# Five blocks of attention and feed-forward on one core: the two P·V steps of a group are set apart, and V's products move between them

## The chip, the cores and the metric

The kernel runs on one core of a Trainium2 chip. The metric is the device time of one execution in microseconds (us), the median of several runs. A profiled execution has a span (first to last instruction) and a time of its own beside it.

## What is computed

Input x has 32 sequences of 64 rows with 128 columns, the context 32 x 64 rows with 96 columns. Five stages follow one another, all in float32:

```python
x = attn(ln(x, g1, b1), ln(x, g1, b1), Wq1, Wk1, Wv1, Wo1, bo1) + x   # SELF: 16 heads of 64
x = attn(ln(x, g2, b2), context, Wq2, Wk2, Wv2, Wo2, bo2) + x         # CROSS: keys and values of the context
x = geglu_ff(ln(x, g3, b3)) + x                                       # GEGLU
# block 2: attention over the context with 16 heads of 8 (CROSS2), then a feed-forward part (FFN)
...
def attn(xq, xc, ...):
    q, k, v = xq @ Wq, xc @ Wk, xc @ Wv       # 16 heads of 64
    P = softmax(q @ k.T * 64 ** -0.5)         # per sequence and head, 64 x 64
    return (P @ v) @ Wo + bo
```

## The kernel before

The 2048 rows are cut into 8 groups of 256 rows, each of T = 2 tiles of 128 rows (two sequences a tile). The stages SELF and CROSS go over the groups one after another. Every engine has its own program, written out in order, and they meet at semaphores alone: an engine does its rows in the order of the code, and a wait at one row holds up everything behind it on that engine. No planner sets the order.

In group s, `one` is the next group and `two` the one after it (a CROSS group follows the last SELF group). TensorE's program of a SELF or CROSS group is: turn P of tile 0 (`turn_step(s, 0)`, 8 transpositions of 128x128), turn the finished output of the group before, turn x (and the context) of `two` (`x_step`), turn P of tile 1, P times V of both tiles (`av_step`, 64 x 64 matmuls, 64 for each tile), three of the four V products of `one` (`val_step`, three float32r matmuls of 512 columns each), the scores of `one` (`scores_step`, 64x64 matmuls), the output projection (`out_step`), the q and k projections of `two` (`proj_step`, 48 matmuls of 256 columns), and the fourth V product of `one`. The high and the low part of float32r operands are multiplied apart, hence the threes.

What comes out of TensorE lies in PSUM. The scores, the turned P and P·V of tile t all use the banks 2t and 2t+1 of `scp`; everything else that is staged (x, projections, V) goes round three banks `stage0` to `stage2`, each of which is free again when the copies of the product three places earlier are done (`stage_for`). ScalarE (ACT) and VectorE (DVE) copy these results to SBUF: of the turned P one bank each (`pt_step`, into `pt`), of V's products 0, 1 and 3 one half each, of V's product 2 both halves by ACT (`copiers`). The softmax of tile t is a chain: DVE takes the maximum (L1298) and subtracts it (L1303), ACT exponentiates (L1071), DVE sums (L1331) and inverts (L1333), GpSimd (POOL) multiplies by the inverse (L1582) and signals `probs`; only then may `turn_step(s, t)` begin. `av_step(s, t)` waits for the V copies of that tile and for both copies into `pt` of that tile.

`Counts` counts the semaphore values in the order of the program, so that it has to be changed along with the engines.

Of the kernel before, what the change touches and what calls it, by code (L numbers as in the profile page):

```python
# [38 lines left out]
SELF, CROSS, GEGLU, CROSS2, FFN = range(5)  # L39
# [54 lines left out]
class Counts:  # L94


    def __init__(self):
        self.total, self.value, self.uses, self.start = {}, {}, [], {}
        self.x(SELF, 0)
        self.p(SELF, 0)  # L100
        self.x(SELF, 1)
        for t in range(T):
            self.softmax(SELF, 0, t)
        self.p(SELF, 1)
        self.vals(SELF, 0, range(4))
        for p in range(PHASES):
            for g in range(GROUPS):
                self.group(p, g)
# [49 lines left out]
    def group(self, p, g):  # L158
        self.start[("act", p, g)] = self.total["act"]
        self.start[("dve", p, g)] = self.total["dve"]  # L160
        self.start[("uses", p, g)] = len(self.uses)
        one, two = Step(p, g).ahead(1), Step(p, g).ahead(2)
        if p in (SELF, CROSS):
            for t in range(T):
                self.turned(p, g, t)
            if one.phase == GEGLU:
                for t in range(T):
                    self.p(GEGLU, 0, (2 + t,))
                    for i in range(2):
                        self.use("av", p, g, 2 * t + i)  # L170
                self.p(GEGLU, 1, (0, 1))
                self.x(GEGLU, 2)
                self.use("down", GEGLU, 0)
                self.p(GEGLU, 1, (2, 3))
            else:
                self.x(two.phase, two.first)
                for i in range(4):
                    self.use("av", p, g, i)
                self.vals(one.phase, one.first, range(3))
                for t in range(T):  # L180
                    self.softmax(one.phase, one.first, t)
                if two.phase == GEGLU:
                    self.vals(one.phase, one.first, (3,))
                    self.x(GEGLU, 1)
                    self.p(GEGLU, 0, (0, 1))
                else:
                    self.p(two.phase, two.first)
                    self.vals(one.phase, one.first, (3,))
            for name in ("out_turned", "out_copied", "out0", "added"):
                self.tick(name, (p, g))  # L190
        elif p == CROSS2:
            last = one.phase != CROSS2
            if g > 0:
                for i in (2, 3):
                    self.use("pt", p, g - 1, i)
            if not last:
                self.qk(p, g + 1)
                self.use("v", p, g + 1)
                if two.phase == CROSS2:
                    self.x(two.phase, two.first)  # L200
            self.tick("scores", (p, g))
            for t in range(T):
                self.softmax(p, g, t)
            for i in (0, 1):
                self.use("pt", p, g, i)
            if g > 0:
                self.use("at", p, g - 1)
                self.use("wo", p, g - 1)
            if not last and two.phase == FFN:
                self.x(two.phase, two.first)  # L210
            for name in ("out0", "norm", "atted"):
                self.tick(name, (p, g))
            if last:
                for i in (2, 3):
                    self.use("pt", p, g, i)
                self.p(one.phase, one.first, (0, 1))
                self.x(two.phase, two.first)
                self.use("at", p, g)
                self.p(one.phase, one.first, (2, 3))
                self.use("wo", p, g)  # L220
        elif (p, g) != (GEGLU, 0):
            if one:
                self.p(one.phase, one.first, (0, 1))
            if two:
                self.x(two.phase, two.first)
            if one and one.phase == p:
                self.p(one.phase, one.first, (2, 3))
            self.use("down", p, g)
# [37 lines left out]
def attention_blocks(nc, w, out):  # L266
# [3 lines left out]
    with ctx:  # L270
# [323 lines left out]
        def _(pe):  # L594
# [315 lines left out]
            def group(s):  # L910
                one, two = s.ahead(1), s.ahead(2)
# [9 lines left out]
                if s.phase in (SELF, CROSS):  # L921
# [4 lines left out]
                    if before:  # L926
                        out_turn_step(before)
                    x_step(two, s)
                    turn_step(s, 1)
                    av_step(s, 0)  # L930
                    av_step(s, 1)
                    val_step(one, range(3), s)
                    scores_step(one, 0)
                    scores_step(one, 1)
                    out_step(s, 0)
# [1 line left out]
                    if two.phase == GEGLU:  # L937
                        val_step(one, (3,), s)
                        x_step(s.ahead(3), s)
                        p_step(two, s, (0, 1))  # L940
                    else:
                        proj_step(two, s)
                        val_step(one, (3,), s)
                elif s.phase == CROSS2:


# [48 lines left out]
            scores_step(Step(SELF, 0), 0, range(6, PAIRS))  # L995
            scores_step(Step(SELF, 0), 1)
            proj_step(Step(SELF, 1), None)
            val_step(Step(SELF, 0), range(4))
            each_group(pe, group)


# [1 line left out]
        def _(sc):  # L1003
# [137 lines left out]
            def group(s):  # L1141
                one, two = s.ahead(1), s.ahead(2)
# [5 lines left out]
                if s.phase in (SELF, CROSS):  # L1148
                    pt_step(s, 0)
                    x_turned_step(two)  # L1150
                    pt_step(s, 1)
                    av_step(s, 0)
                    av_step(s, 1)
                    val_step(one, range(3))
                    x_high_step(two)
                    for key, first in (("q", 3), ("k", 4), ("v", 5)):
                        if s.is_group(SELF, first):
# [10 lines left out]
                    if two.phase == GEGLU:  # L1168
                        val_step(one, (3,))
                        exp_step(one, 1)  # L1170
                    else:
                        p_step(two, range(2))
                        exp_step(one, 1)
                        p_step(two, range(2, 8))
                        val_step(one, (3,))
                elif s.phase == CROSS2:
                    before, last = s.before(), one.phase != CROSS2
                    if before:
# [43 lines left out]
            p_step(Step(SELF, 1), range(1, 5))  # L1222
            exp_step(Step(SELF, 0), 1)
            p_step(Step(SELF, 1), range(5, 8))
            val_step(Step(SELF, 0), range(4))
            each_group(sc, group)


        @block.vector
        def _(ve):  # L1230
# [174 lines left out]
            def group(s):  # L1405
# [7 lines left out]
                if s.phase in (SELF, CROSS):  # L1413
# [5 lines left out]
                    pt_step(s, 0)  # L1419
                    if before:  # L1420
                        out_step(before)
                    pt_step(s, 1)
                    stats_step(three)
                    av_step(s, 0)
                    av_step(s, 1)
                    val_step(one, (0,))
                    max_step(one, 0)
                    shift_step(one, 0)
                    if two.phase != GEGLU:
# [6 lines left out]
                    if two.phase == GEGLU:  # L1436
                        probs_step(one, 0)
                    sum_step(one, 1)
                    if two.phase != GEGLU:
                        val_step(one, (3,))  # L1440
                    if three.is_group(GEGLU, 0):
                        stats_step(s.ahead(4))
                elif s.phase == CROSS2:
# [60 lines left out]
            sum_step(Step(SELF, 0), 0)  # L1504
            p_step(Step(SELF, 1), range(4, 8))
            sum_step(Step(SELF, 0), 1)
            val_step(Step(SELF, 0), range(4))
            each_group(ve, group, looks_far=True)


# [199 lines left out]
```

## Time and profile before

| | |
|---|---|
| median of 3 runs | 456.05 us (454.42 to 456.29) |
| profiled execution: time / span | 456.08 us / 454.4 us |
| TensorE busy | 438.6 us, 97% of the span |
| VectorE, ScalarE, GpSimd busy | 355.0 us (78%), 320.0 us (70%), 198.1 us (44%) |
| granted TensorE clock | 1.00 |

The share of busy time is an average over the whole span. SELF and CROSS together take the part from about 26 to 302 us.

### The profile page before, as it was taken

How to read it: one execution, taken by the hardware profiler on the slowest of the kernel's cores; microseconds unless marked ns; L12 is line 12 of the kernel's file. 1: busy time of each engine (PE TensorE's matmuls, PEld its weight loads, DVE VectorE, ACT ScalarE, POOL GpSimd, SP SyncE). 2: the span in 40 equal slices, each digit the busy share in tenths (PEclk: the TensorE clock that was granted, in tenths of full speed). 3: DMA queues.
4: the chain of work that ended last, by engine and by line, in shares of the span. 5: the costliest groups of instructions: out<-in, count | busy, mean ns of one | idle time of the engine just before them, and what ended most of it. 6: DMA issues, size and time to landing. Idle time of an engine off the chain costs nothing.

```text
span 454.4 us, 17380 instructions
## 1 busy us (share of the span) xinstructions
PE 438.6 (97%) x7545; PEld 403.5 (89%) x7545; DVE 355.0 (78%) x653; ACT 320.0 (70%) x589; POOL 198.1 (44%) x220
## 2 busy tenths in 40 slices
PE   7999999999999999999999999999999999999897
PEld 7979999898998999999989899888999777877797
DVE  4888889688797897887968879896774787898571
ACT  5686676776878768777776777875565576766763
POOL 2793332565455535553354433533332231232583
PEclk9999999999999999999999999999999999999999
DMA  7102021110200000000000000000000000000011
GB/s 227 47 15 84 3 84 30 50 48 7 60 3 4 10 12 2 12 3 10 12 4 10 3 12 12 4 1 1 3 0 19 10 20 11 0 1 3 13 36 46
DMA packets 14621, 10.57 MB, mean 23 GB/s; under 512 B 5188, under 2 KB 13592, under 8 KB 14552
## 3 DMA queue, kind: packets, MB, share of 16 engines
q1 hardware_dynamic: 14120, 9.48, 7.3%
q8 instruction: 56, 0.92, 0.8%
q10 hardware_dynamic: 432, 0.07, 0.1%
q14 instruction: 13, 0.11, 0.1%
HBM read 8.50 MB, written 1.05 MB: 21 GB/s over the span
## 4 chain that ended last, share of the span: by engine, by line
PE 85%; DVE 7%; ACT 4%; issue 2%; DMA 1%; POOL 0%; DVEq 0%; ACTq 0%; POOLq 0%
PE stage L637 12%; PE stage L638 11%; PE stage L639 11%; PE scp L812 7%; PE scp L733 7%; PE scp L886 6%; PE scp L782 6%; PE out0p L832 4%; PE out0p L834 3%; PE out0p L833 3%; PE out0p L858 3%; PE stage L796 2%; PE scp L750 2%; DVE pr L1303 1%; DVE mx L1298 1%
## 5 line engine op out<-in xcount | busy, mean ns | idle before, releaser
L1582 POOL TENSOR_TENSOR pr<-pr,rc 128x1024 f32<-128x1024 f32 (+1 forms) x32 | 59.1, 1866 | 76.9 <-DVE rc L1333 76.8
L1071 ACT ACTIVATE pr<-pr 128x1024 f32<-128x1024 f32 x48 | 50.8, 1059 | 37.7 <-DVE pr L1303 29.9
L1521 POOL TENSOR_TENSOR rstd<-veps,neghalf 128x2 f32<-128x2 f32 x32 | 22.7, 710 | 78.0 <-DVE veps L1251 77.9
L1005 ACT ACTIVATE vt<-stage 64x512 f32<-64x512 f32 x83 | 49.2, 592 | 4.7 <-PE stage L639 1.2
L1347 DVE COPY vt<-stage 64x512 f32<-64x512 f32 x45 | 31.2, 694 | 21.8 <-PE stage L639 20.9
L1298 DVE TENSOR_REDUCE mx<-scp 128x16 f32<-128x1024 f32 x32 | 39.2, 1224 | 9.0 <-PE scp L733 8.5
L1005 ACT ACTIVATE ot_h<-scp 128x512 fp32r<-128x512 f32 x64 | 33.5, 601 | 13.4 <-PE scp L812 13.4
L1353 DVE TENSOR_TENSOR ot_r<-scp,ot_h 128x512 fp32r<-128x512 f32 x64 | 40.0, 684 | 2.4 <-ACT ot_h L1005 1.0
L1005 ACT ACTIVATE k_of_heads<-stage 128x512 f32<-128x512 f32 x62 | 36.9, 597 | 5.6
L1303 DVE TENSOR_TENSOR pr<-scp,mx 128x1024 f32<-128x1024 f32 x32 | 39.2, 1225 | 1.1
L1331 DVE TENSOR_REDUCE sm<-pr 128x16 f32<-128x1024 f32 x32 | 38.0, 1188 | 0.0
L812 PEld LDWEIGHTS scp<-pt,vt 64*64 64x64 f32 x2048 | 32.4, 135 | 5.9 <-issue 5.6
L812 PE MATMUL scp<-pt,vt 64*64 64x64 f32 x2048 | 34.9, 221 | 2.7 <-issue 1.6
L733 PEld LDWEIGHTS scp<-k_of_heads,q_of_heads 64*64 64x64 f32 x2048 | 31.5, 135 | 6.2 <-issue 5.7
L733 PE MATMUL scp<-k_of_heads,q_of_heads 64*64 64x64 f32 x2048 | 33.9, 220 | 0.6 <-issue 0.6
L782 PE MATMUL scp<-ident,pr 128*128 128x128 f32 x256 | 33.7, 274 | 0.2 <-POOL pr L1582 0.2
L1595 POOL TENSOR_TENSOR masked_k<-kT,fourmask 128x1024 f32<-128x1024 f32 x8 | 15.1, 1893 | 42.9 <-ACT kT L1050 42.9
L1005 ACT ACTIVATE q_of_heads<-stage 128x512 f32<-128x512 f32 x49 | 27.5, 589 | 7.5 <-PE stage L639 7.0
L782 PEld LDWEIGHTS scp<-ident,pr 128*128 128x128 f32 x256 | 29.0, 140 | 3.2 <-POOL pr L1582 0.5
L1358 DVE COPY pt<-scp 128x512 f32<-128x512 f32 x32 | 22.1, 692 | 9.6 <-PE scp L782 9.6
L1005 ACT ACTIVATE pt<-stage 128x512 f32<-128x512 f32 x32 | 17.9, 595 | 9.3 <-PE stage L796 8.7
L1537 POOL TENSOR_TENSOR rows<-rows,bias 128x256 f32<-128x256 f32 (+1 forms) x32 | 23.3, 731 | 1.2
(257 smaller groups left out, 1408.9 us busy)
## 6 DMA issues: line engine op xcount, KB each, us to landing
ctx_in<-in_ctx_dram SPq DMA_DIRECT2D x16, 96.0 KB, 2.0
masked_k<-in_L_xattn_Wo_dram SPq DMA_DIRECT2D x2, 512.0 KB, 3.8
out_dram<-rows SPq DMA_DIRECT2D x8, 128.0 KB, 1.8
rows<-in_x_dram SPq DMA_DIRECT2D x1, 768.0 KB, 9.5
pr<-in_L_xattn_Wq_dram SPq DMA_DIRECT2D x1, 512.0 KB, 4.6
pr<-in_L_xattn_Wk_dram SPq DMA_DIRECT2D x1, 512.0 KB, 6.2
pt<-in_L_xattn_Wv_dram SPq DMA_DIRECT2D x1, 512.0 KB, 7.6
rows<-in_L_xattn_Wq_dram SPq DMA_DIRECT2D x1, 512.0 KB, 3.7
```

Source lines behind the costliest of these rows:

```text
L637: nc.tensor.matmul(dst, wh, mh, start=start, stop=False)
L638: nc.tensor.matmul(dst, wh, mr, start=False, stop=False)
L639: return nc.tensor.matmul(dst, wr, mh, start=False, stop=True)
L733: last = nc.tensor.matmul(scp[64 * b:64 * b + 64, 2 * t + e, a * N:(a + 1) * N], heads_of[0][h, a, n], heads_of[1][h, a, n], start=True, s ...
L782: last = nc.tensor.transpose(scp[:, 2 * t + c, q * 128:(q + 1) * 128], pr[t][:, a * 128:(a + 1) * 128], ident[:, :])
L812: last = nc.tensor.matmul(banks[i][64 * e:64 * e + 64, m * ROWS + b * N:m * ROWS + (b + 1) * N], vt[h, 2 * t + b, (2 * m + e) * DH:(2 * m ...
L1005: return nc.scalar.activation(dst, s, ACT.Copy)
L1071: nc.scalar.activation(pr[t][:, :], pr[t][:, :], ACT.Exp, scale=scale[s.phase]).then_inc(exped, 1)
L1298: nc.vector.tensor_reduce(mx[:, t, :], sc3, AX.X, ALU.max).then_inc(maxed, 1)
L1303: nc.vector.tensor_tensor(halves(pr[t][:, :]), sc3, mx[:, t, :, None].to_broadcast([ROWS, H, N]), ALU.subtract).then_inc(shifted, 1)
L1353: nc.vector.tensor_tensor(ot_r[:, :, i, t, :], bank, of.bitcast(F32), ALU.subtract).then_inc(dve, 1)
L1582: nc.gpsimd.tensor_tensor(p, p, rc[:, t, h:, None].to_broadcast([ROWS, H - h, N]), ALU.mult)\
```

## The change

The fourth V product of a group, which stood at the end of the group before, now stands inside its own group, behind the turn of `two`'s x. P·V of tile 0 follows it; only then comes the turn of P of tile 1, then the first V product of the next group, P·V of tile 1, and the V products 1 and 2. The last SELF/CROSS group that uses this code (CROSS, 6) keeps its successor's fourth product where it was. ACT and DVE copy in the new order; on DVE the statistics of group `three` move ahead of the second copy of the turned P. No instruction is added to any engine and none is removed.

```diff
--- before.py
+++ after.py
@@ -102,7 +102,7 @@
         for t in range(T):
             self.softmax(SELF, 0, t)
         self.p(SELF, 1)
-        self.vals(SELF, 0, range(4))
+        self.vals(SELF, 0, range(3))
         for p in range(PHASES):
             for g in range(GROUPS):
                 self.group(p, g)
@@ -174,9 +174,12 @@
                 self.p(GEGLU, 1, (2, 3))
             else:
                 self.x(two.phase, two.first)
+                self.vals(p, g, (3,))
                 for i in range(4):
+                    if i == 2:
+                        self.vals(one.phase, one.first, (0,))
                     self.use("av", p, g, i)
-                self.vals(one.phase, one.first, range(3))
+                self.vals(one.phase, one.first, (1, 2))
                 for t in range(T):
                     self.softmax(one.phase, one.first, t)
                 if two.phase == GEGLU:
@@ -185,7 +188,6 @@
                     self.p(GEGLU, 0, (0, 1))
                 else:
                     self.p(two.phase, two.first)
-                    self.vals(one.phase, one.first, (3,))
             for name in ("out_turned", "out_copied", "out0", "added"):
                 self.tick(name, (p, g))
         elif p == CROSS2:
@@ -926,10 +928,12 @@
                     if before:
                         out_turn_step(before)
                     x_step(two, s)
+                    val_step(s, (3,), s)
+                    av_step(s, 0)
                     turn_step(s, 1)
-                    av_step(s, 0)
+                    val_step(one, (0,), s)
                     av_step(s, 1)
-                    val_step(one, range(3), s)
+                    val_step(one, (1, 2), s)
                     scores_step(one, 0)
                     scores_step(one, 1)
                     out_step(s, 0)
@@ -940,7 +944,6 @@
                         p_step(two, s, (0, 1))
                     else:
                         proj_step(two, s)
-                        val_step(one, (3,), s)
                 elif s.phase == CROSS2:
 
 
@@ -995,7 +998,7 @@
             scores_step(Step(SELF, 0), 0, range(6, PAIRS))
             scores_step(Step(SELF, 0), 1)
             proj_step(Step(SELF, 1), None)
-            val_step(Step(SELF, 0), range(4))
+            val_step(Step(SELF, 0), range(3))
             each_group(pe, group)
 
 
@@ -1148,10 +1151,12 @@
                 if s.phase in (SELF, CROSS):
                     pt_step(s, 0)
                     x_turned_step(two)
+                    val_step(s, (3,))
                     pt_step(s, 1)
                     av_step(s, 0)
+                    val_step(one, (0,))
                     av_step(s, 1)
-                    val_step(one, range(3))
+                    val_step(one, (1, 2))
                     x_high_step(two)
                     for key, first in (("q", 3), ("k", 4), ("v", 5)):
                         if s.is_group(SELF, first):
@@ -1172,7 +1177,6 @@
                         p_step(two, range(2))
                         exp_step(one, 1)
                         p_step(two, range(2, 8))
-                        val_step(one, (3,))
                 elif s.phase == CROSS2:
                     before, last = s.before(), one.phase != CROSS2
                     if before:
@@ -1222,7 +1226,7 @@
             p_step(Step(SELF, 1), range(1, 5))
             exp_step(Step(SELF, 0), 1)
             p_step(Step(SELF, 1), range(5, 8))
-            val_step(Step(SELF, 0), range(4))
+            val_step(Step(SELF, 0), range(3))
             each_group(sc, group)
 
 
@@ -1419,11 +1423,12 @@
                     pt_step(s, 0)
                     if before:
                         out_step(before)
+                    val_step(s, (3,))
+                    stats_step(three)
                     pt_step(s, 1)
-                    stats_step(three)
                     av_step(s, 0)
+                    val_step(one, (0,))
                     av_step(s, 1)
-                    val_step(one, (0,))
                     max_step(one, 0)
                     shift_step(one, 0)
                     if two.phase != GEGLU:
@@ -1436,8 +1441,6 @@
                     if two.phase == GEGLU:
                         probs_step(one, 0)
                     sum_step(one, 1)
-                    if two.phase != GEGLU:
-                        val_step(one, (3,))
                     if three.is_group(GEGLU, 0):
                         stats_step(s.ahead(4))
                 elif s.phase == CROSS2:
@@ -1504,7 +1507,7 @@
             sum_step(Step(SELF, 0), 0)
             p_step(Step(SELF, 1), range(4, 8))
             sum_step(Step(SELF, 0), 1)
-            val_step(Step(SELF, 0), range(4))
+            val_step(Step(SELF, 0), range(3))
             each_group(ve, group, looks_far=True)
```

On TensorE, group SELF 6 (V's products read `wv_of0`, here `src0` for the group's own product 3 and `src1` for those of SELF 7), from the last V product ahead of the turns to the scores. Before:

```order
L637 MATMUL stage<-wv_of0h,src0h 128x512
L638 MATMUL stage<-wv_of0r,src0h 128x512
L639 MATMUL stage<-wv_of0h,src0r 128x512
L782 MATMUL scp<-ident,pr 128x128 x8
L843 MATMUL out0p<-ident,attT 128x128 x2
L648 MATMUL stage<-ident,ctx_in 96x128 x2
L655 MATMUL stage<-ident,xn 128x128 x2
L782 MATMUL scp<-ident,pr 128x128 x8
L812 MATMUL scp<-pt,vt 64x64 x64
L637 MATMUL stage<-wv_of0h,src1h 128x512
```

The same place in the changed kernel (its lines are numbered two higher):

```order
L784 MATMUL scp<-ident,pr 128x128 x8
L845 MATMUL out0p<-ident,attT 128x128 x2
L650 MATMUL stage<-ident,ctx_in 96x128 x2
L657 MATMUL stage<-ident,xn 128x128 x2
L639 MATMUL stage<-wv_of0h,src0h 128x512
L640 MATMUL stage<-wv_of0r,src0h 128x512
L641 MATMUL stage<-wv_of0h,src0r 128x512
L814 MATMUL scp<-pt,vt 64x64 x32
L784 MATMUL scp<-ident,pr 128x128 x8
L639 MATMUL stage<-wv_of0h,src1h 128x512
L640 MATMUL stage<-wv_of0r,src1h 128x512
L814 MATMUL scp<-pt,vt 64x64 x32
```

The first turn now follows the projections at once, and the one run of 64x64 matmuls (a row of this view counts them by twos: x64 stands for 128) is now two runs, with 128x128 matmuls between them.

On VectorE, the same group, from the last reciprocal of SELF 6's softmax to the first maximum of SELF 7's. Before:

```order
L1333 RECIPROCAL rc<-sm 128x16
L1347 COPY vt<-stage 64x512
L1358 COPY pt<-scp 128x512
L1365 TENSOR_TENSOR rows<-out0p,rows 128x256
L1358 COPY pt<-scp 128x512
L1242 BN_STATS stats<-rows 128x6 x2
L1246 COPY seen<-stats 128x1
L1248 BN_AGGR mv<-stats 128x2 x2
L1251 TENSOR_SCALAR veps<-mv 128x2
L1353 TENSOR_TENSOR ot_r<-scp,ot_h 128x4x128 x4
L1347 COPY vt<-stage 64x512
L1298 TENSOR_REDUCE mx<-scp 128x16
```

In the changed kernel, from behind the reciprocal (its lines are numbered four higher):

```order
L1362 COPY pt<-scp 128x512
L1369 TENSOR_TENSOR rows<-out0p,rows 128x256
L1351 COPY vt<-stage 64x512
L1246 BN_STATS stats<-rows 128x6 x2
L1250 COPY seen<-stats 128x1
L1252 BN_AGGR mv<-stats 128x2 x2
L1255 TENSOR_SCALAR veps<-mv 128x2
L1362 COPY pt<-scp 128x512
L1357 TENSOR_TENSOR ot_r<-scp,ot_h 128x4x128 x2
L1351 COPY vt<-stage 64x512
L1357 TENSOR_TENSOR ot_r<-scp,ot_h 128x4x128 x2
L1302 TENSOR_REDUCE mx<-scp 128x16
```

The copy of the V product and the statistics now stand ahead of the second copy into `pt`, and another V copy stands between the two pairs of P·V's remainders.

## Rows read from the trace of the kernel before

**Rows 1.** The page: the chain that ended last, share of the span by engine

```profile
PE 85%; DVE 7%; ACT 4%; issue 2%; DMA 1%; POOL 0%; DVEq 0%; ACTq 0%; POOLq 0%
```

**Rows 2.** Busy time by group: window, length, each engine's us (instructions), clock, DMA

```profile
81.35:100.82 19.47, 18.80 (x363) 17.29 (x361) 15.45 (x25) 14.34 (x26) 9.57 (x9) 1.00 0.11 33
100.82:119.84 19.02, 18.43 (x362) 17.06 (x360) 15.45 (x25) 14.33 (x25) 9.69 (x9) 1.00 0.14 39
119.84:137.97 18.13, 18.13 (x362) 16.95 (x361) 15.36 (x25) 14.15 (x25) 9.41 (x9) 1.00 0.01 3
137.97:156.32 18.35, 18.35 (x364) 17.17 (x362) 15.35 (x25) 14.71 (x27) 10.21 (x10) 1.00 0.04 8
...
229.76:249.27 19.51, 18.62 (x364) 17.30 (x363) 15.46 (x25) 14.01 (x26) 7.86 (x9) 1.00 0.03 8
249.27:268.07 18.80, 18.52 (x364) 17.18 (x363) 15.45 (x25) 13.91 (x26) 7.97 (x9) 1.00 0.03 8
```

**Rows 3.** Timeline of TensorE, group SELF 6: start, length, line, operation

```profile
137.27 0.40 PE L637 MATMUL stage<-wv_of0h,src0h 128*128 128x512 f32 x1
...
137.97 1.03 PE L782 MATMUL scp<-ident,pr 128*128 128x128 f32 x8
138.84 0.38 PE L843 MATMUL out0p<-ident,attT 128*128 128x128 f32 x2
...
139.49 1.04 PE L782 MATMUL scp<-ident,pr 128*128 128x128 f32 x8
140.46 2.12 PE L812 MATMUL scp<-pt,vt 64*64 64x64 f32 x128
142.51 0.50 PE L637 MATMUL stage<-wv_of0h,src1h 128*128 128x512 f32 x1
142.85 0.39 PE L638 MATMUL stage<-wv_of0r,src1h 128*128 128x512 f32 x1
143.08 0.40 PE L639 MATMUL stage<-wv_of0h,src1r 128*128 128x512 f32 x1
...
144.46 0.39 PE L639 MATMUL stage<-wv_of0h,src1r 128*128 128x512 f32 x1
144.78 2.10 PE L733 MATMUL scp<-k_of_heads,q_of_heads 64*64 64x64 f32 x128
...
156.32 1.03 PE L782 MATMUL scp<-ident,pr 128*128 128x128 f32 x8
```

**Rows 4.** Timeline of VectorE, group SELF 6

```profile
140.57 0.69 DVE L1358 COPY pt<-scp 128x512 f32<-128x512 f32 x1 [0.51 <-PE scp L782]
141.17 0.48 DVE L1242 BATCH_NORM_STATS2 stats<-rows 128x6 f32<-128x128 f32 x2
...
142.03 0.17 DVE L1251 TENSOR_SCALAR veps<-mv 128x2 f32<-128x2 f32 x1
...
146.01 1.23 DVE L1298 TENSOR_REDUCE mx<-scp 128x16 f32<-128x1024 f32 x1 [0.50 <-PE scp L733]
...
153.49 0.25 DVE L1333 RECIPROCAL rc<-sm 128x16 f32<-128x16 f32 x1
...
156.52 0.69 DVE L1347 COPY vt<-stage 64x512 f32<-64x512 f32 x1 [1.41 <-PE stage L639]
```

**Rows 5.** Timeline of GpSimd: one product by the inverse, and a pair of them

```profile
135.47 1.90 POOL L1582 TENSOR_TENSOR pr<-pr,rc 128x1024 f32<-128x1024 f32 x1 [4.00 <-DVE rc L1333]
...
153.82 3.77 POOL L1582 TENSOR_TENSOR pr<-pr,rc 128x1024 f32<-128x1024 f32 x2 [3.25 <-DVE rc L1333]
```

**Rows 6.** Timeline of two places where TensorE waited: CROSS 6 and CROSS 7

```profile
288.39 0.69 DVE L1358 COPY pt<-scp 128x512 f32<-128x512 f32 x1
...
289.23 0.47 PE L812 MATMUL scp<-pt,vt 64*64 64x64 f32 x17 [0.41 <-DVE pt L1358]
...
301.28 1.55 POOL L1582 TENSOR_TENSOR pr<-pr,rc 128x512 f32<-128x512 f32 x1 [4.60 <-DVE rc L1333]
...
302.89 0.33 PE L782 MATMUL scp<-ident,pr 128*128 128x128 f32 x1 [0.24 <-POOL pr L1582]
```

## The prediction, made before the changed kernel ran

> **What bounds the kernel now.** I read the chain that ended last first: 85% of it is TensorE [rows 1]. An average can hide stages, so the busy time by group comes next: in the groups of SELF and CROSS from 119.84 and from 137.97, TensorE's busy time is the whole window (18.13 of 18.13 us, 18.35 of 18.35), while VectorE has 15.36 and 15.35 and the others less [rows 2]. At full clock throughout, every us added to TensorE's stream there is a us of the kernel, and there are next to no waits left to take away. The exceptions are four groups with pauses, which the profile puts down to issue and not to another engine: 19.47 and 19.02 against 18.13, 19.51 and 18.80 against 18.35, together 3.8 us [rows 2].
>
> A second loop runs close behind it. From the start of the scores (144.78) TensorE comes to the next turn at 156.32, 11.54 us later [rows 3]. The softmax of tile 0 goes the same way round: the maximum starts at 146.01, the reciprocal at 153.49 [rows 4], GpSimd at 153.82, and one product by the inverse takes 1.90 [rows 5]; so P of tile 0 is ready at 155.72, and TensorE takes up such a result 0.06 us after it (301.28 + 1.55 = 302.83, and the turn starts at 302.89) [rows 6]. That makes 155.78, or 11.00 us after the start of the scores: 0.54 us of cover. VectorE's share of this can't shrink, since it works through from the maximum to the sums, and the change leaves its rows there in their order.
>
> **The change, term by term, in one group.** The instructions are the same 364, so only their neighbours and the waits change.
>
> 1. The switch between 128x128 and 64x64 matmuls. The eight turns of tile 0 take 0.87 us to the next row (137.97 to 138.84), the eight of tile 1, with P·V behind them, 0.97 (139.49 to 140.46): 0.10 for going into 64x64. Behind P·V the first V matmul takes 0.34 to the next (142.51 to 142.85) where the second takes 0.23: 0.11 for coming out. V to scores is the same again, 0.32 against 0.23 [rows 3]. Before there are two runs of 64x64 matmuls in a group, P·V and scores; after there are three, as P·V is cut in two. One way in and one way out more: 0.21 us. The program has no semaphore ahead of that first V matmul that was late, so a wait doesn't explain the 0.11.
>
> The Trainium skill (TensorEngine Tiling (Array Packing), Key Properties) says that changing the tiling mode, not just the tile, drains TensorE. By that rule the switch costs in both directions, as these rows show; taken as a whole turn in flight on the way in, it would be 0.16 (a turn is 0.27 us long and follows the last in 0.11) in place of my 0.10, and the 15 groups would cost 0.9 us more. The rows measure the switch itself, so the sum goes by them.
>
> 2. P·V of tile 1 waits for the copy of its turned P. The copy by VectorE starts 1.08 us after the start of turn 1 (139.49 to 140.57) and takes 0.69 [rows 4]; a P·V that was held up by such a copy starts 0.15 behind its end (288.39 + 0.69 = 289.08, and 289.23) [rows 6]. So P·V of tile 1 can't start before 1.92 us after turn 1, besides the 0.11 of the switch ahead of that turn, which is counted in term 1. TensorE has 0.87 of turns and one V product between, 0.70 (137.27 to 137.97), and 0.10 for the switch: 1.67 [rows 3]. The wait is 0.25 us. Before, 64 matmuls of P·V of tile 0, 1.0 us, were the cover, plus the switch; the V product alone is 0.3 shorter. The copy must also find VectorE free. Ahead of it stand now the V copy and the statistics. By the rows, the V product ends 2.22 us after turn 0 (1.52 + 0.70), its copy at about 3.1, the statistics take 1.03 (141.17 to 142.20) and end at 4.1, and the copy is due at 4.5. That fits by 0.4. The P·V copies of tile 1 end at about 8.4 after turn 0, the second scores need them at 9.0, and the maximum starts at 9.2: no new wait there.
>
> 3. The first turn waits for `probs`. With the fourth V product gone from its front, TensorE reaches it 11.54 - 0.70 = 10.84 us after the scores, and P is ready after 11.00: 0.16 us of wait. The wait stands first in the group, so all of TensorE's work of the group is behind it. Turn 1, on the other hand, comes 1.8 us later than before while its P is ready 1.87 after tile 0's: no wait.
>
> 4. The V product itself moves by 0.70 us inside the loop and costs the same. Its bank needs the copies of the projection three places earlier, and VectorE had idled 1.41 us ahead of its copy [rows 4]: nothing is late.
>
> A second way to the same sum is the loop: turn 0 to scores was 6.81 (137.97 to 144.78) and becomes 6.81 + 0.70 + 0.21 + 0.25 = 7.97; scores to turn 0 becomes 11.00. The group is 18.97 us where it was 18.35: +0.62. The new waits add up and don't cover one another, since each is met at another place of one loop.
>
> **The sum.** Terms 1 and 2 fall in 15 groups (SELF 0 to 7, CROSS 0 to 6): 15 x 0.46 = 6.9. Term 3 falls in the 14 of them that follow another: 14 x 0.16 = 2.2. Back come the 0.41 us that TensorE waited in CROSS 6 [rows 6], where the copy of turned P stood behind the statistics and a V copy that is gone now. In SELF 0 two small waits may change places; I count nothing. Together +8.7. The profiled execution has 456.08 us (span 454.4), which is the median of the runs (456.05), so the forecast is 465.
>
> **Bounds.** Term 1 is measured four times and lies between 0.18 and 0.24: 2.7 to 3.6. Term 2 is nothing if VectorE's copy starts earlier than before relative to its turn (0), and 0.4 if VectorE is late by as much again; I take 0.25 because start and length of the copy are the same operation on the same tile. Term 3 is nothing if anything speeds up the chain by 0.16, and 0.3 if GpSimd's signal takes as long to act as VectorE's 0.15. All at the low end: +2.3 to +2.7; all at the high end: about +13.
>
> **The rivals.**
> (a) Only the switches count: a moment's slack in the two waits that I work out to tenths. For it: 0.25 and 0.16 are differences of large numbers. Against it: they come from the same steady loop, repeated 14 times. 15 x 0.21 gives 3.2, less 0.4: 459. Chance 0.17.
> (b) The pauses go. They fall into or right after the dense runs of 64x64 matmuls, and these are now shorter. With my terms: 465 - 3.8 = 461. For it: 128 matmuls in a run are 64 now. Against it: the scores keep their run, and two of the four pauses (100.82, 249.27) are not in P·V's share of their group as far as I can tell from windows. Chance 0.12.
> (c) The other side, faster: the same pauses go and the switch and both waits are hidden, 456.1 - 3.8 - 0.4 = 452. It decides only from the point at which the added cost of a group is below 0.13 us (15 x 0.13 = 2, and 0.5% is 2.3 us); one switch each way is more than that already. Chance 0.04.
> (d) No difference: P·V behind a semaphore that is met late hides its own switch, and somewhere 0.4 us of a group is given back that I don't see: 456. Chance 0.07.
> (e) More: VectorE, moved closer to its limit, delays the second copy or the scores by another 0.3 us in each group, 15 x 0.3 = 4.5: 469. It decides if the statistics end later than 4.5 us after turn 0, 0.4 more than worked out. Chance 0.08.
> The forecast itself has 0.52, with a range of 462 to 467.5.
>
> **How the numbers follow.** The range 459 to 468 holds the forecast, (b) and most of (a), and leaves out (c), (d) and most of (e). A measurement of this kernel tells about 0.5%, 2.3 us, from no change. Faster by more: (c), 0.04. Within: (d) and the low part of (a), 0.10. Slower: the rest, 0.86.
>
> **What would show it.** Right: groups of about 18.9 to 19.0 us from turn 0 to turn 0; three places in a group where TensorE's pitch has the extra 0.1; P·V of tile 1 with a wait on VectorE's copy into `pt`; the first turn of a group with a short wait on GpSimd; TensorE's busy share below that of before. Wrong: first turns that follow the projections without a gap (term 3), P·V of tile 1 that starts 1.7 us after turn 1 (term 2), no extra pitch at the second run of 64x64 (term 1), or groups without pauses at all (b).

## The result, and the profile after

The changed kernel takes 464.11 us (463.72 to 464.22, 4 runs) against 455.64 (454.42 to 456.29, 4 runs) on the same chip: 1.0187 of the time before, 95% interval 1.0163 to 1.0211. That is 8.5 us slower; 465 was forecast, in a range of 459 to 468.

The page of the changed kernel, its chain that ended last, answers to [rows 1]:

```profile
span 462.4 us, 17382 instructions
...
PE 445.4 (96%) x7545; PEld 401.9 (87%) x7545; DVE 359.6 (78%) x653; ACT 320.7 (69%) x589; POOL 198.2 (43%) x220
...
PE 80%; DVE 13%; ACT 3%; issue 2%; DMA 1%; POOL 0%; DVEq 0%; ACTq 0%; POOLq 0%
```

TensorE is still the bound, but VectorE's share of the chain is 13% where it was 7%: TensorE now waits for it in every group. The span is 8.0 us longer.

Busy time by group in the changed kernel, from turn 0 to turn 0, answers to [rows 2]:

```profile
82.84:102.04 19.20, 19.03 (x362) 17.00 (x362) 15.53 (x25) 14.34 (x25) 9.56 (x9) 1.00 0.12 40
102.04:121.43 19.39, 18.82 (x360) 17.02 (x360) 15.63 (x25) 14.32 (x24) 9.55 (x9) 1.00 0.14 38
121.43:140.34 18.91, 18.74 (x363) 16.90 (x361) 15.53 (x25) 14.24 (x25) 9.56 (x9) 1.00 0.01 3
140.34:159.44 19.10, 18.93 (x363) 17.11 (x363) 15.53 (x25) 14.83 (x26) 10.23 (x10) 1.00 0.03 8
255.07:274.17 19.10, 18.91 (x362) 17.10 (x363) 15.53 (x25) 13.87 (x25) 7.87 (x9) 1.00 0.03 8
```

A regular group that turns a context (SELF 6 to CROSS 5) takes 19.10 us instead of 18.35, one without takes 18.90 instead of 18.20. The long groups with pauses, up to 19.5 us before, are nearly gone: the longest is the one of 19.39 us.

The timeline of TensorE in SELF 6 of the changed kernel answers to [rows 3]:

```profile
140.34 1.09 PE L784 MATMUL scp<-ident,pr 128*128 128x128 f32 x8
141.27 0.38 PE L845 MATMUL out0p<-ident,attT 128*128 128x128 f32 x2
...
142.38 0.40 PE L641 MATMUL stage<-wv_of0h,src0r 128*128 128x512 f32 x1
142.71 1.16 PE L814 MATMUL scp<-pt,vt 64*64 64x64 f32 x64
143.80 1.09 PE L784 MATMUL scp<-ident,pr 128*128 128x128 f32 x8
144.65 0.49 PE L639 MATMUL stage<-wv_of0h,src1h 128*128 128x512 f32 x1
144.98 0.39 PE L640 MATMUL stage<-wv_of0r,src1h 128*128 128x512 f32 x1
145.21 0.40 PE L641 MATMUL stage<-wv_of0h,src1r 128*128 128x512 f32 x1
145.77 1.16 PE L814 MATMUL scp<-pt,vt 64*64 64x64 f32 x64 [0.17 <-DVE pt L1362]
146.86 0.50 PE L639 MATMUL stage<-wv_of0h,src1h 128*128 128x512 f32 x1
...
148.43 2.10 PE L735 MATMUL scp<-k_of_heads,q_of_heads 64*64 64x64 f32 x128
```

Turn 0 to scores is 8.09 us (140.34 to 148.43), where 7.97 was forecast. The second P·V starts 0.56 us after the last V matmul (145.21 to 145.77) instead of the 0.33 that stand ahead of the first one (142.38 to 142.71): 0.23 of wait. And each half of P·V takes 1.09 us (142.71 to 143.80, 145.77 to 146.86), together 0.13 more than the undivided 2.05 (140.46 to 142.51) of [rows 3]. The eight turns of tile 0 take 0.93 us to their successor (140.34 to 141.27) instead of 0.87.

The timelines of VectorE and of GpSimd in the same group answer to [rows 4, 5]:

```profile
144.41 0.17 DVE L1255 TENSOR_SCALAR veps<-mv 128x2 f32<-128x2 f32 x1
144.94 0.69 DVE L1362 COPY pt<-scp 128x512 f32<-128x512 f32 x1 [0.35 <-PE scp L784]
...
149.66 1.23 DVE L1302 TENSOR_REDUCE mx<-scp 128x16 f32<-128x1024 f32 x1 [0.72 <-PE scp L735]
...
157.15 0.25 DVE L1337 RECIPROCAL rc<-sm 128x16 f32<-128x16 f32 x1
```

```profile
157.48 3.76 POOL L1585 TENSOR_TENSOR pr<-pr,rc 128x1024 f32<-128x1024 f32 x2 [3.08 <-DVE rc L1337]
```

The second copy of turned P starts as soon as its turn is over: VectorE has been idle for 0.35 us, so the statistics in front of it hold up nothing. It ends at 145.63, 0.14 ahead of the second P·V. GpSimd's first product ends 1.90 us after 157.48, at 159.38, and the next first turn starts 0.06 later, at 159.44: scores to turn is 11.01 us, bound by the softmax.

### The profile page after: what moved, and what is told of

Its sections match the earlier page's. It is cut to its first block, busy times and chain, and to the rows that moved or that the text cites. A ratio compares the mean times of both kernels' runs of the same rounds, so it can differ in the third digit from the quotient of the medians.

```text
span 462.4 us, 17382 instructions
## 1 busy us (share of the span) xinstructions
PE 445.4 (96%) x7545; PEld 401.9 (87%) x7545; DVE 359.6 (78%) x653; ACT 320.7 (69%) x589; POOL 198.2 (43%) x220
## 4 chain that ended last, share of the span: by engine, by line
PE 80%; DVE 13%; ACT 3%; issue 2%; DMA 1%; POOL 0%; DVEq 0%; ACTq 0%; POOLq 0%
PE stage L639 11%; PE stage L641 10%; PE stage L640 10%; PE scp L814 7%; PE scp L784 7%; PE scp L735 6%; PE scp L888 6%; PE out0p L834 3%; PE out0p L860 3%; PE out0p L835 3%; PE out0p L836 3%; DVE pt L1362 3%; PE stage L798 2%; PE scp L752 2%; DVE pr L1307 2%
## 5 line engine op out<-in xcount | busy, mean ns | idle before, releaser
L1357 DVE TENSOR_TENSOR ot_r<-scp,ot_h 128x512 fp32r<-128x512 f32 x64 | 41.2, 685 | 0.5
L814 PE MATMUL scp<-pt,vt 64*64 64x64 f32 x2048 | 37.2, 221 | 4.2 <-DVE pt L1362 3.4
L1008 ACT ACTIVATE ot_h<-scp 128x512 fp32r<-128x512 f32 x64 | 34.7, 597 | 6.9 <-PE scp L814 6.9
L784 PE MATMUL scp<-ident,pr 128*128 128x128 f32 x256 | 35.1, 280 | 0.4 <-POOL pr L1585 0.2
L784 PEld LDWEIGHTS scp<-ident,pr 128*128 128x128 f32 x256 | 27.5, 140 | 4.6 <-POOL pr L1585 2.9
L1008 ACT ACTIVATE pt<-scp 128x512 f32<-128x512 f32 x32 | 19.1, 597 | 16.8 <-PE scp L784 15.9
L1551 POOL TENSOR_TENSOR src1r<-xT,src1h 128x256 fp32r<-128x256 f32 x16 | 12.1, 754 | 29.4 <-ACT src1h L1008 17.5
```

What stands on the lines that cost most here:

```text
L784: last = nc.tensor.transpose(scp[:, 2 * t + c, q * 128:(q + 1) * 128], pr[t][:, a * 128:(a + 1) * 128], ident[:, :])
L814: last = nc.tensor.matmul(banks[i][64 * e:64 * e + 64, m * ROWS + b * N:m * ROWS + (b + 1) * N], vt[h, 2 * t + b, (2 * m + e) * DH:(2 * m ...
L1008: return nc.scalar.activation(dst, s, ACT.Copy)
L1357: nc.vector.tensor_tensor(ot_r[:, :, i, t, :], bank, of.bitcast(F32), ALU.subtract).then_inc(dve, 1)
```

## The experiments

The times below are medians against the kernel before, run on the same chip.

**e1: the fourth V product moved, nothing else.**

```diff
                     x_step(two, s)
+                    val_step(s, (3,), s)
                     turn_step(s, 1)
                     av_step(s, 0)
                     av_step(s, 1)
                     val_step(one, range(3), s)
...
                         proj_step(two, s)
-                        val_step(one, (3,), s)
```

> Only the fourth V product moves into its own group; both turns, P times V undivided and the V products 0 to 2 stand as before. Theory (wait on probs is real): groups with 64x64 runs as before, first turn waits about 0.16 to 0.25 us for GpSimd in 14 groups, so a regular CROSS group is 18.5 to 18.6 us instead of 18.35, and the time is 2.2 to 3.3 us above before, less 0.4 in CROSS 6. Rival (the wait costs nothing, all of the loss is the split): 18.35 per group and no change. On the pauses: if the shorter runs of 64x64 matmuls took them away in the changed kernel, this one keeps them (3 to 4 us in groups of over 18.8 us); if the place of the V product did, they are gone here and the time comes out near that of before or below.

457.86 us, 1.0049 (1.0032 to 1.0067). The timeline of TensorE, a row from a pause, the scores in SELF 6 and the turn that follows them:

```profile
91.54 0.57 PE L733 MATMUL scp<-k_of_heads,q_of_heads 64*64 64x64 f32 x22 [0.62 <-issue]
...
145.46 2.09 PE L733 MATMUL scp<-k_of_heads,q_of_heads 64*64 64x64 f32 x128
156.47 1.09 PE L782 MATMUL scp<-ident,pr 128*128 128x128 f32 x8
```

Scores to turn is 11.01 us again, the same as in the changed kernel, and a group is 18.57 (137.90 to 156.47) instead of 18.35, in CROSS 18.55: the wait on `probs` is there with P·V undivided. The group grows by about 0.21 us, 0.05 more than the wait of 11.00 - 10.84, because the turns of tile 0 take 0.93 to their successor instead of 0.87. That isn't part of the wait (see e6). The pauses stay, 2.4 us.

**e2: P·V divided, nothing else.** Both turns stay ahead of it, so that neither copy is late.

```diff
                     av_step(s, 0)
+                    val_step(one, (0,), s)
                     av_step(s, 1)
-                    val_step(one, range(3), s)
+                    val_step(one, (1, 2), s)
```

> Only P times V is divided, with V's first product between the halves; both turns stay ahead of the first half and the fourth V product stays behind the projections, so neither new wait can arise. Theory (two more switches and the start of one more run cost 0.21 to 0.34 us a group): regular CROSS group 18.56 to 18.69 us, 3.2 to 5.1 us in all, less what pauses give back (up to 3.8). Rival (the switch is free and all of the loss of the changed kernel is its two waits): 18.35 us a group. If division takes the pauses away, groups are all regular and the time is only 0 to 2 us above before.

458.72 us, 1.0065 (1.0051 to 1.0079). The timeline of TensorE in one group:

```profile
178.91 1.16 PE L814 MATMUL scp<-pt,vt 64*64 64x64 f32 x64
180.00 0.50 PE L639 MATMUL stage<-wv_of1h,ctx_src1h 96*128 96x512 f32 x1
180.34 0.40 PE L640 MATMUL stage<-wv_of1r,ctx_src1h 96*128 96x512 f32 x1
180.58 0.40 PE L641 MATMUL stage<-wv_of1h,ctx_src1r 96*128 96x512 f32 x1
180.90 1.16 PE L814 MATMUL scp<-pt,vt 64*64 64x64 f32 x64
182.00 0.50 PE L639 MATMUL stage<-wv_of1h,ctx_src1h 96*128 96x512 f32 x1
```

No row has a wait. A group is 18.70 us: 0.35 more, of which 0.09 go into the second run (0.32 where the pitch is 0.23), 0.11 come out of the first, and the halves take 1.09 and 1.10 where half of 2.05 is 1.03: 0.07 each. The starts of the single matmuls in the trace show where that goes: inside a run 16 matmuls take 0.23 us, but the first 16 of every run take 0.28 and the last 16 about 0.34 to the next instruction. These 0.05 and 0.11 are met once a run, long or short, so a run more costs them once more. 15 x 0.35 is 5.2 us, but the time rose by 3.2: the pauses shrank from 3.8 us to 2.0 (groups of 19.19, 19.22 and 19.33 us are left).

**e3: the turns of the context and of x as cover for the second copy**, in the changed kernel.

```diff
-                    x_step(two, s)
                     val_step(s, (3,), s)
                     av_step(s, 0)
                     turn_step(s, 1)
+                    x_step(two, s)
                     val_step(one, (0,), s)
                     av_step(s, 1)
```

> The changed kernel with the turns of the context and of x put between turn 1 and V's first product, as cover for the second copy of turned P. Theory (the wait on that copy is real, 0.22 us a group, and separate from the switch): no wait in front of the second P times V, turn 0 to scores 7.87 us instead of 8.09, 15 x 0.22 = 3.3 us below the changed kernel, about 460.8. Rival (the wait only moves: the loop through VectorE, ScalarE and GpSimd is bound elsewhere, or P times V of tile 0 now waits): same time as the changed kernel, 463 to 465.

461.56 us, 1.0131 (1.0113 to 1.0148), 2.5 below the changed kernel. A group is 18.90 us (215.20 to 234.10), turn 0 to scores 7.90: the wait on the second copy is real and costs 0.20 us a group.

**e4: VectorE's copy of V product 1 ahead of the first maximum**, in the changed kernel.

```diff
                     val_step(one, (0,))
                     av_step(s, 1)
+                    if two.phase != GEGLU:
+                        val_step(one, (1,))
                     max_step(one, 0)
                     shift_step(one, 0)
-                    if two.phase != GEGLU:
-                        val_step(one, (1,))
                     max_step(one, 1)
```

> The changed kernel with VectorE's copy of V product 1 ahead of the first maximum instead of behind it; VectorE idles 0.72 us there. Theory (the first turn waits for the chain through probs): the chain is 0.5 to 0.7 us shorter, the wait of 0.16 to 0.22 us in front of the first turn is gone in 14 groups, and so is the 0.1 us that TensorE loses in the k projections to a late q copy: 2.2 to 4.5 us below the changed kernel, 460 to 462. Rival (the first turn's late start is something else, such as the time to start behind the projections): no change, 464.

461.52 us, 1.0128 (1.0110 to 1.0146), 2.6 below the changed kernel. The timeline of VectorE:

```profile
147.51 0.70 DVE L1351 COPY vt<-stage 64x512 f32<-64x512 f32 x1
148.24 1.23 DVE L1302 TENSOR_REDUCE mx<-scp 128x16 f32<-128x1024 f32 x1
149.50 1.22 DVE L1307 TENSOR_TENSOR pr<-scp,mx 128x1024 f32<-128x1024 f32 x1
150.64 1.21 DVE L1302 TENSOR_REDUCE mx<-scp 128x16 f32<-128x1024 f32 x1
```

The copy fills what was 0.72 us of idling, the maximum starts hardly later after the scores (146.98 to 148.24, 1.26 instead of 1.23), and scores to turn falls to 10.77 us, below the 10.84 that TensorE needed in the forecast, because the next lost tenth goes too (see e5). A group is 18.90. The gain of 0.20 is thus the wait on `probs` together with that lost tenth, not the wait alone.

**e5: the same move of one copy in the kernel before.** The diff is that of e4.

> The kernel before, with only VectorE's copy of V product 1 ahead of the first maximum. The first maximum may start up to 0.2 us later, the second one and everything behind it 0.5 us earlier. Theory (TensorE loses 0.1 us a group at the sixth product of the q and k projections to a q copy that ScalarE makes behind the second exponential): that 0.1 goes in 14 groups, 1.0 to 1.5 us, about 454.3. Rival (the first turn already had cover and that 0.1 is no wait): no change, 455.6.

454.25 us, 0.9973 (0.9960 to 0.9985): faster than before, by 0.3%. The kernel before, TensorE's timeline at the change from q to k projections:

```profile
153.25 0.28 PE L639 MATMUL stage<-ctx_src0h,wk_of1r 96*128 96x256 f32 x1
153.36 0.38 PE L637 MATMUL stage<-ctx_src0h,wk_of1h 96*128 96x256 f32 x1
153.58 0.28 PE L638 MATMUL stage<-ctx_src0r,wk_of1h 96*128 96x256 f32 x1
```

and this kernel's:

```profile
152.43 0.28 PE L639 MATMUL stage<-ctx_src0h,wk_of1r 96*128 96x256 f32 x1
152.55 0.28 PE L637 MATMUL stage<-ctx_src0h,wk_of1h 96*128 96x256 f32 x1
152.67 0.28 PE L638 MATMUL stage<-ctx_src0r,wk_of1h 96*128 96x256 f32 x1
```

The second maximum on VectorE, in the kernel before and in this one:

```profile
149.25 1.23 DVE L1298 TENSOR_REDUCE mx<-scp 128x16 f32<-128x1024 f32 x1
```

```profile
147.86 1.21 DVE L1298 TENSOR_REDUCE mx<-scp 128x16 f32<-128x1024 f32 x1
```

Before, the sixth projection's first matmul took 0.22 us to the next where the pitch is 0.12; now it is in step. Its bank waits for the third projection's copy, which ScalarE makes behind the second exponential; the second maximum now starts 3.90 us after the scores (143.96 to 147.86) instead of 4.47 (144.78 to 149.25), and that goes through to the copy. A group is 18.25 instead of 18.35.

**e6: e1 with the copy moved.** The diffs of e1 and e4 together.

> The run with only the fourth V product moved, and VectorE's copy of V product 1 ahead of the first maximum. Theory (the move costs only the wait on probs, and that wait is a matter of VectorE's order): groups of 18.3 to 18.4 us, 2 to 3 us below the run without the copy moved, 455 to 456, level with before. Rival (the moved product costs in its own place too): 0.1 us a group or more above that, 457.

455.29 us, 1.0006 (0.9991 to 1.0021); a group is 18.31 us. The timeline of TensorE, the first turns of CROSS 1:

```profile
192.15 1.09 PE L782 MATMUL scp<-ident,pr 128*128 128x128 f32 x8
193.08 0.38 PE L843 MATMUL out0p<-ident,attT 128*128 128x128 f32 x2
```

These turns start 0.15 us after the last projection matmul (192.00), where in e1 it is 0.28 (193.40 to 193.68): the wait is gone. They still take 0.93 to their successor. In e5, where a V product stands ahead of them, they take 0.88 (192.04 to 192.92). Against e5, which has the same copy moved, a group is 0.06 us longer. So the moved V product does cost something in its new place, about 0.06 us a group, since the turns now follow the projections; the other 0.16 that e1 lost was the wait, a matter of VectorE's order.

**e7: e3 with the copy moved**, both remedies in the changed kernel.

> The changed kernel with both remedies: turns of x as cover for the second copy of turned P, and VectorE's copy of V product 1 ahead of the first maximum. Theory (both waits are separate and add up, only the divided run of P times V is left): 18.70 us a group, as in the run with the division alone, 464.1 - 2.5 - 2.6 = 459. Rival (the two waits cover one another): 461.5, no better than each alone.

458.62 us, 1.0075 (1.0062 to 1.0087); a group is 18.67 us. The two remedies add up (19.10 - 0.20 - 0.20 = 18.70). What is left over e6, the same without the division, is 0.36 us a group: the division again, 0.35 in e2.

**e8: the scores divided instead of P·V**, in the kernel before; on TensorE alone.

```diff
-                    val_step(one, range(3), s)
+                    val_step(one, (0, 1), s)
                     scores_step(one, 0)
+                    val_step(one, (2,), s)
                     scores_step(one, 1)
```

> The kernel before with V product 2 between the scores of tile 0 and those of tile 1: TensorE's rows alone change, and it is the scores that are divided. Theory (a divided run of 64x64 matmuls costs 0.35 us wherever it stands, and dividing also gives back pauses): 18.70 us a group, 5.2 us less 1 to 3 of pauses, 458 to 460. Rival (the price belongs to P times V, its four semaphore waits among it): 18.35 to 18.5 us a group.

459.72 us, 1.0095 (1.0080 to 1.0110). A regular group is 18.64 us, 0.29 more than before; the price of a division is nearly the same at another place of the program and doesn't belong to P·V. The second half of what was expected failed: the pauses didn't shrink. The waits of TensorE from 40 to 300 us put down to issue:

```profile
PE scp L812 <- issue: 1.6, 2, 0.9
PE scp L733 <- issue: 0.5, 1, 0.5
```

**e0: the kernel before once more.**

> The kernel before once more, for its pauses. If they belong to the program, they stand at the same places in the second trace (groups from about 81, 101, 230 and 249 us, 3.8 us in all); if they are chance, places and sum differ.

One execution, 455.22 us. Its timeline of TensorE, the rows with pauses:

```profile
86.49 0.45 PE L812 MATMUL scp<-pt,vt 64*64 64x64 f32 x11 [0.63 <-issue]
110.01 0.32 PE L733 MATMUL scp<-k_of_heads,q_of_heads 64*64 64x64 f32 x2 [0.57 <-issue]
234.90 0.27 PE L812 MATMUL scp<-pt,vt 64*64 64x64 f32 x2 [0.68 <-issue]
```

In the first trace three of the four pauses stand at these very matmuls (11 before the end of P·V, 2 before the end of the scores, 2 before the end of P·V), the fourth is missing here, and the long groups sum to 3.1 us more instead of 3.8. So they belong to the program, with some chance in the last one and in the lengths.

The place can be said more closely. In the trace of the kernel before, the four pauses come after 3009, 4033, 8897 and 9921 of TensorE's instructions, counted from the start (weight loads, matmuls and its few others). These counts are multiples of 256 apart. The first three return in e0, and in all 13 traces every gap of over 0.4 us from 40 to 300 us that isn't a wait on another engine's result lies a multiple of 256 from them. The page has a row that fits:

```profile
q8 instruction: 56, 0.92, 0.8%
```

These are 56 transfers of instructions, about one for every 270 of TensorE's instructions, so the pauses seem to stand where one block of the program ends and the next begins.

**e9: the statistics of GEGLU 1 later**, in the changed kernel. The forecast had 0.41 us coming back in CROSS 6, and that didn't come: turn 0 to scores is 8.44 there against 8.11 in a regular group, where before it was 7.28 and 7.15 (e0) against 6.80. VectorE's timeline there in the changed kernel, and GpSimd's:

```profile
293.33 1.79 DVE L1255 TENSOR_SCALAR veps<-mv 128x2 f32<-128x2 f32 x1
295.04 0.68 DVE L1362 COPY pt<-scp 128x512 f32<-128x512 f32 x1
```

```profile
291.33 3.76 POOL L1585 TENSOR_TENSOR pr<-pr,rc 128x1024 f32<-128x1024 f32 x2 [5.47 <-DVE rc L1337]
```

An addition over 128x2 elements took 1.79 us instead of 0.17 and ended at 295.12, 0.03 after GpSimd's two products (295.09); the first copy of turned P stood behind it. The edit moves the statistics behind that copy:

```diff
                     pt_step(s, 0)
                     if before:
                         out_step(before)
+                    if s.is_group(CROSS, GROUPS - 2):
+                        stats_step(s.ahead(3))
...
-                    if three.is_group(GEGLU, 0):
-                        stats_step(s.ahead(4))
```

> The changed kernel with the statistics of GEGLU 1 behind the first copy of turned P of CROSS 6 instead of ahead of it. Theory (that copy is late because the statistics' last operation runs beside GpSimd's product and ends only with it, 1.79 us instead of 0.17): the operation is 0.2 us or so again, and turn 0 to scores in CROSS 6 falls from 8.44 to 7.9 or 8.0 us. Rival (P times V of CROSS 6 is late for another reason): 8.4 us stay. The time changes by half a us at most.

One execution, 464.42 us. VectorE's and then TensorE's timeline:

```profile
296.02 0.17 DVE L1255 TENSOR_SCALAR veps<-mv 128x2 f32<-128x2 f32 x1
...
298.47 0.69 DVE L1362 COPY pt<-scp 128x512 f32<-128x512 f32 x1
```

```profile
299.30 1.16 PE L814 MATMUL scp<-pt,vt 64*64 64x64 f32 x64 [1.15 <-DVE pt L1362]
```

The addition, now behind the end of GpSimd's products, takes 0.17 us, as expected; but turn 0 to scores in CROSS 6 went up, from 8.44 to 8.88, and not down to 7.9 or 8.0 as expected: two sets of statistics now stand ahead of the second copy of turned P, and the second P·V waits 1.15 us for it.

**e10: e5 with the statistics later.** The diffs of e4 and e9 in the kernel before.

> The kernel before with both moves on VectorE: the copy of V product 1 ahead of the first maximum, and the statistics of GEGLU 1 behind the first copy of turned P of CROSS 6. Turn 0 to scores in CROSS 6 from 7.15 to about 6.65 us; against the run with the first move alone 0.4 to 0.5 us less, 453.8, which the timing can't tell from it; against before 0.3 to 0.4% less. If the late statistics hold up the start of GEGLU, it comes out at or above 454.25.

454.38 us, 0.9975 (0.9964 to 0.9987): level with e5. Turn 0 to scores in CROSS 6 is 7.13 us, as without the move (7.15); the wait went from the first P·V to the second. The expected 0.5 us isn't there.

## Why the prediction was right, and where it was not

The direction and the three mechanisms held; that the total came out within a microsecond was in part luck. The terms were these, for one group and then for the kernel:

| term | forecast | measured | by |
|---|---|---|---|
| 1, the division of P·V | 0.21, x 15 | 0.35 | e2, e7 against e6; 0.29 for the scores in e8 |
| 2, the wait on the second copy | 0.25, x 15 | 0.20 | e3 |
| 3, the wait on `probs` | 0.16, x 14 | 0.16 | e1 |
| the turns of tile 0 behind the projections | 0 | 0.05, x 14 | e1, e6 |
| sum of a group | 0.62 | 0.75 | 19.10 - 18.35 (the terms give 0.76) |
| pauses, in all | 0 | -2.9 | 3.8 before, 0.9 after |
| CROSS 6 | -0.4 | none seen | rows above |

15 x 0.35 + 15 x 0.20 + 14 x 0.21 = 11.2 us, less 2.9 of pauses, is 8.3; the spans differ by 8.0. The point forecast was close because two errors of two to three us stood against each other: the groups cost 11.2 us instead of 9.1, and the pauses gave back what the forecast had left in place. That is luck.

**Term 1 was mis-sized.** The forecast read the pitch at the borders of the runs and took 0.18 to 0.24 as bounds. Going in and coming out are as read, 0.09 and 0.11. The borders don't show what a run costs inside, the slower first and last 16 of its matmuls: 2 x 1.09 against 2.05 is 0.13 to 0.14 more. The rule of the Trainium skill that a change of tiling mode drains TensorE (TensorEngine Tiling (Array Packing), Key Properties) fits in direction, and e2 and e8 show a price with no late semaphore; the rows can't tell a drain from other reasons for it.

**Terms 2 and 3** came out by the method: add the producer's start and length, and compare with TensorE's own rows. Both are separate, as the forecast said; e3, e4 and e7 take away one, the other, and both. Under point 4 the forecast held that the V product costs the same in its new place. It costs 0.05 to 0.06 us more there, waited for or not (0.93 instead of 0.87 for the turns that follow the projections, e6). And the forecast's remark that VectorE's share of the softmax can't shrink was wrong: the copy of V product 1, 0.70 us long, stood between the first subtraction and the second maximum, and moving it away shortened the chain (e4, e5).

**The pauses** were left unchanged in the forecast and went largely away: rival (b), given 0.12, happened beside the forecast, not instead of it. The sums, each from the lengths of groups against the regular one, are 3.8 and 3.1 (before, twice), 2.4 (e1), 3.8 (e8), 2.0 (e2), 1.2 (e7), 0.9 (after). e7 has neither of the two waits and still few pauses, so it isn't the waits that hide them; e8 has a run divided and all of them, so it isn't division as such. They shrink where P·V is divided. The counts of e0 say something on why. In the kernel before, the stretches of 256 instructions that end at the four pauses took 3.0, 2.6, 2.1 and 2.5 us; no other from 40 to 300 us took less than 3.4. In the changed kernel the stretches that end at 3009 and 8897 take 4.6 and 3.8 us, and their pauses are gone; the one that ends at 4033 takes 2.6 and keeps its pause. That fits a next block of instructions that comes late when the one before is run through fast. It isn't shown: the stretch that ends at 9921 takes 2.4 us in the changed kernel and has no pause, and no run tried it by itself.

**The 0.41 us in CROSS 6** rested on the statistics taking 1.03 us. With the V copy gone from their front they started earlier, and beside GpSimd's products one of their operations took ten times as long. The forecast didn't ask what they would now run beside. All 13 traces together show that this is no chance. This addition occurs 416 times in them; 28 times it began while an operation of GpSimd was running, and each time it ended 0.02 to 0.03 us after that operation, whether it took 0.20 us or 1.79. The other 388 took 0.17. The Trainium skill (GPSIMD Engine Reference, 1. Specifications) says that GpSimd's SBUF interfaces are shared with VectorE and contended by some of its instructions; the 28 ends agree with that, and 0.17 us in e9, after the products had ended, does too. That VectorE waits for GpSimd's operation to end is shown; that it does so at a shared interface is the page's account.

## What to carry to other kernels

On an engine that is the bound, count not only what each instruction costs but how often its kind changes (here between 64x64 and 128x128 matmuls), and measure a run's length as a whole: half a run is more than half its time. When a product is taken out of the space between a producer and a wait, subtract it from the cover (here 0.54 us of cover and 0.70 taken away) before calling the move free, and look first at the order of copies on the helper engines: one copy moved into VectorE's idle time ahead of the maximum gave 0.3%, which none of TensorE's orders did. A small gain counted on from an earlier start needs the question what the operation will then run beside.

## What the runs showed of the hardware that wasn't expected

- A 64x64 run of 64 matmuls takes 1.09 us, one of 128 takes 2.05.
- A VectorE addition over 128x2 elements took 1.79 us (0.17 elsewhere) and ended 0.03 us after GpSimd's multiplication that ran beside it; in SELF 0 of the changed kernel the same operation has 1.40. All 28 such additions that began beside a GpSimd operation ended 0.02 to 0.03 us after it.
- Eight 128x128 turns take 0.93 us to their successor behind projection matmuls of 256 columns (0.90 in CROSS 0), whether they were waited for (e1) or not (e6), and 0.87 behind a V product of 512.
- Pauses of 0.3 to 0.9 us that the profile puts down to issue stand at the same matmuls in two executions of one program, each a multiple of 256 of TensorE's instructions from the others, and shrink with the order of the code.
